# Combine rows behind every third gather instead of every second, with a small GpSimd write behind each gather

## What is computed

```python
x = x + 0.5 * ffn(layernorm(x))
x = x + attn(layernorm(x))          # einsum, softplus, exp, scan over time, einsum
x = x + 0.5 * ffn(layernorm(x))

def ffn(x):                          # 16 experts, 4 taken per token
    weights, indices = top_k(sigmoid(gate_w @ x) + gate_b, 4)
    weights = weights / weights.sum(-1)
    shared = silu(x @ w1s) * (x @ w3s) @ w2s
    for the four chosen experts e of a token:
        routed += weights[e] * (silu((x @ w1[e]) * (x @ w3[e])) @ w2[e])
    return shared + routed
```

## Time and profile before

| what | value |
|---|---|
| time, median of 3 runs | 590.1 us (585.19 to 593.1) |
| span of the profiled execution | 644.2 us |
| mean granted TensorE clock in it | 0.897 |
| busy: TensorE, VectorE, ScalarE, GpSimd | 517.4, 434.0, 376.0, 349.6 us |
| first and last x gather of loop 0 | 75.97 and 246.85 us |
| first and last x gather of loop 1 | 405.81 and 576.18 us |
| gathers issued by GpSimd | 158 of x, 64 early rows, 64 late rows |

### The profile page before, as it was taken

The page is one execution under the profiler, slowest core; times in us unless marked ns, Lnnn a source line. Parts: engine busy times, 40 slices in busy tenths (PEclk is TensorE's granted clock), DMA queues, the critical chain, the costliest instruction groups (busy, mean ns, idle before and its releaser), DMA issues.

```text
span 644.2 us, 13458 instructions
## 1 busy us (share of the span) xinstructions
PE 517.4 (80%) x3206; PEld 454.5 (71%) x3207; DVE 434.0 (67%) x1459; ACT 376.0 (58%) x1128; POOL 349.6 (54%) x364
## 2 busy tenths in 40 slices
PE   4976799999999999667586943799999899998460
PEld 3954589998888889455465931599988788887350
DVE  6798667767767677527686689467666667666434
ACT  2778466766657567555474664477766666665010
POOL 3899554456556565465311442544565556655764
PEclk9978589999999999697697975599999999999875
DMA  9971245565444445432100560254444454555644
GB/s 297 391 269 68 60 130 156 163 179 153 151 145 135 147 129 138 126 95 79 53 2 0 167 210 0 66 150 133 132 150 131 132 149 130 145 137 142 190 129 121
DMA packets 61149, 88.24 MB, mean 137 GB/s; under 512 B 9499, under 2 KB 46363, under 8 KB 61107
## 3 DMA queue, kind: packets, MB, share of 16 engines
q1 hardware_dynamic: 47379, 50.29, 22.7%
q0 software_dynamic: 13728, 37.50, 22.6%
HBM read 57.22 MB, written 30.54 MB: 136 GB/s over the span
## 4 chain that ended last, share of the span: by engine, by line
PE 56%; DVE 11%; issue 10%; ACT 9%; POOL 5%; another core or an unknown queue 4%; DMA 4%; SPq 1%; ACTq 0%; POOLq 0%; DVEq 0%
PE bank L1380 24%; PE bank L1431 10%; PE bank L1402 6%; POOL mamba_room L595 5%; PE bank L1442 4%; PE bank L1441 4%; PE bank L1599 2%; DMA ys_scratch<-ring_f 2%; PE bank L1488 2%; ACT ring_f L713 1%; ACT ring_r L664 1%; DVE xres L1159 1%; PE bank L1624 1%; PE bank L1453 1%
## 5 line engine op out<-in xcount | busy, mean ns | idle before, releaser
L560 POOL DMA_INDIRECT ring_f<-xn_scratch,tokidx x158 | 149.6, 947 | 153.0 <-PE bank L1402 100.6
L1380 PE MATMUL bank<-w_routed,ring_r 128*128 x948 | 195.5, 342 | 0.9 <-DVE ring_r L954 0.8
L1380 PEld LDWEIGHTS bank<-w_routed,ring_r 128*128 128x128 f32 x948 | 152.2, 192 | 6.6 <-issue 4.1
L1431 PE MATMUL bank<-w_routed,ring_r 128*128 x790 | 119.5, 281 | 3.0 <-ACT ring_f L692 2.1
L1431 PEld LDWEIGHTS bank<-w_routed,ring_r 128*128 128x128 f32 x790 | 110.0, 188 | 4.3 <-issue 4.3
L673 ACT ACTIVATE ring_r<-bank 128x256 fp32r<-128x256 f32 x158 | 60.7, 384 | 71.4 <-PE bank L1442 66.5
L962 DVE TENSOR_TENSOR ring_r<-bank,ring_r 128x128 fp32r<-128x128 f32 x158 | 45.6, 288 | 59.9 <-ACT ring_r L673 47.4
L595 POOL DMA_INDIRECT mamba_room<-ys_scratch,si x64 | 61.6, 962 | 29.1 <-issue 18.4
L954 DVE TENSOR_TENSOR ring_r<-bank,ring_r 128x256 fp32r<-128x256 f32 x158 | 67.1, 425 | 15.1 <-issue 5.4
L1402 PE MATMUL bank<-cst,ring_f 128*128 128x128 f32 x316 | 64.4, 286 | 10.0 <-DMA ring_f<-xn_scratch,tokidx 5.4
L682 ACT ACTIVATE stage<-bank 128x176 f32<-128x176 f32 x158 | 50.6, 320 | 35.7 <-remote 18.2
(11 more groups left out here) (172 smaller groups left out, 816.5 us busy)
## 6 DMA issues: line engine op xcount, KB each, us to landing
ys_scratch<-ring_f SPq DMA_DIRECT2D x158, 128.0 KB
raw_routed<-in_w13r SPq DMA_DIRECT2D x6, 704.0 KB, 12.5
xn_scratch<-w_routed SPq DMA_DIRECT2D x32, 128.0 KB, 4.9
raw_routed<-in_w2r SPq DMA_DIRECT2D x6, 512.0 KB, 12.8
raw_routed<-in_w13r SPq DMA_DIRECT2D x8, 352.0 KB, 6.4
ring_f<-xn_scratch,tokidx POOLq DMA_INDIRECT x158
xres<-in_x_in SPq DMA_DIRECT2D x4, 512.0 KB, 6.4
raw_routed<-in_w2r SPq DMA_DIRECT2D x8, 256.0 KB, 6.7
```

The lines of the kernel that those rows point to most:

```text
L560: pool.indirect_dma_start(xg[j % UN], None, xn_dram, bass.IndirectOffsetOnAxis(ap=tokidx[:, j:j + 1], axis=0)).then_inc(s_g[j % UN], 16)
L1380: last = pe.matmul(out, a, b, start=(q == 0), stop=(q == len(terms) - 1))
L1431: last = pe.matmul(p_y[b][:, 0:D], a, v, start=(q == 0), stop=(q == 4))
```

## The change

There are four parts.

1. `EARLY_TURN = 3`: early fetch n stands behind gather 29 + 3n instead of 29 + 2n.
2. `space`: from gather 25 on (`SPACED_FROM`), GpSimd writes 64 columns of zeros into `hid_room`, whose contents are no longer needed then, behind each x gather and behind each early fetch inside the loop. Each such write waits for the one before it, on a new semaphore that nothing else uses. Fetches behind the loop have none.
3. `MEASURED = 4`: one token tile fewer is measured inside the loop.
4. `measure_early` moves from the list's stage with lag 0 to that with lag 3, with the step number adjusted, so that it can still be reached in the steps after the last gather.

```diff
-EARLY_FIRST, EARLY_ADD = 29, 3
+EARLY_FIRST, EARLY_ADD, EARLY_TURN = 29, 3, 3
+SPACED_FROM, SPACE = EARLY_FIRST - 4, 64
-MEASURED = 5
+MEASURED = 4
...
-            return max(4 * (n // TOPK) + EARLY_FIRST, EARLY_FIRST + 2 * n)
+            return max(4 * (n // TOPK) + EARLY_FIRST, EARLY_FIRST + EARLY_TURN * n)
...
+            spaces = [0]
+
+            def space(j):
+
+                if j >= SPACED_FROM:
+                    if spaces[0]:
+                        pool.wait_ge(s_sp, spaces[0])
+                    spaces[0] += 1
+                    pool.memset(hid_room[:, 0:SPACE], 0.0).then_inc(s_sp, 1)
...
                 for j in range(NS):
                     gather(f, j)
+                    space(j)
                     for n in range(EARLY):
                         if early_after(n) == j:
                             fetch_early(f, n)
+                            space(j)
...
-                        if c == early_step(t * TOPK + TOPK - 1) + 1:
+                        if c + LAG_T + 1 == early_step(t * TOPK + TOPK - 1) + 1:
                             mark(measured(t))
-                    if f == 0 and c == early_step(SCALED[0][1] * TOPK - 1) + 3:
+                    if f == 0 and c + LAG_T + 1 == early_step(SCALED[0][1] * TOPK - 1) + 3:
...
-                                   (LAG_X, dve_x(base)), (LAG_X, shared_rows_first(f)), (LAG_X, measure_early(f))],
+                                   (LAG_X, dve_x(base)), (LAG_X, shared_rows_first(f)), (LAG_T + 1, measure_early(f))],
```

More of the change, by code:

```diff
@@ L296, in build @@
         s_ea = sem("early_added")
+        s_sp = sem("spaced")
         s_wo = sem("mamba_out_loaded")
```

## The result

| | median | lowest to highest | ratio to before (95% interval) |
|---|---|---|---|
| before | 590.88 us (4 runs) | 585.19 to 593.1 | |
| changed | 609.58 us (4 runs) | 607.54 to 611.89 | 1.0336 (1.0294 to 1.0377) |

The changed kernel is slower by 19 to 20 us. The forecast was 593 us, "that gain and loss nearly cancel", with 573 to 611 us as the range: the time lies inside the range, near its upper end, but outside the 582 to 602 us of the likeliest case. It lies 1.6 us from the 608 us of rival C.

The account below looks back on a forecast made before the run. Fetches in the loops were taken to make GpSimd's gathers delay TensorE's signals, 2.36 instead of 2.00 us per tile. Terms -19.7 + 20.0 + 2.0 + 0.4 = +2.7 on 590.1 gave 593 us, range 573 to 611 us.

Parts of the forecast that it names:

- likeliest case: Whole kernel: gain in the loops and loss behind them nearly cancel, 582 to 602 us; chance 0.38.
- rival C: Loops: late signals belong to the profiled execution, little to gain, eight more fetches behind each loop cost about +18, 608 us; chance 0.14.
- The pace of the loops, -19.7 us: Gathers 29 to 78, both loops: 2.16 instead of 2.36 us per tile, 9.5 and 10.2 us less.
- rival B: Loop rounds: zeros don't part the gathers, TensorE's signals stay held, the train of eight costs too; +20.5, 611 us; chance 0.16.
- GpSimd's 1.41 us per gather: GpSimd: a gather takes about 1.41 us though issued 1.25 us apart; three or more in succession delay TensorE's signals.
- the pace of 2.16 us per tile: Loops: GpSimd sets the pace, four gathers with zeros at 1.62 us each per three tiles.
- The zeros at 0.21 us: GpSimd in the loops: a write of 64 columns of zeros takes 0.21 us, between 0.10 and 0.54.
- The fetches behind the loops, +20.0 us: Behind each loop: eight more fetches in a row at 1.25 us, 10.0 us later each; not below 16.
- The train of eight at the loops' ends, +2.0 us: Each loop's end: gathers 77, 78 and fetches 16 to 21 hold TensorE's signals, up to 6 us, taken as 1 each.
- The one more statistic, +0.4 us: Behind loop 0: one more statistic is left to compute there, +0.4 us.
- A: Loops: spaced gathers keep signals prompt, zeros are short, 2.00 us per tile; -15.1, 575 us; chance 0.29.
- D: Loops: zeros take 0.54 us or more, GpSimd holds 2.60 us per tile; +24 + 20, 634 us; chance 0.03.

Follow-up runs that it names:

- before_again: The kernel before, unchanged, profiled a second time: 590.86 us, ratio 1.0035.
- before_third: The kernel before, unchanged, profiled a third time: 592.11 us (1 run).
- open_all: The kernel before with fetch n behind gather 29 + 5n/3 and, in layer 1, no fetch waits for TensorE's tiles or shared sums: 578.76 us, ratio 0.9782.

## Why the prediction went as it did

**The pace of the loops, -19.7 us: wrong, it was nothing.** The rows were read rightly: in that execution TensorE's signals were late. The step that failed is the last one of the sum, "Carried over as it is, the forecast is 590.1 + 2.7". The span was 54 us above the median, the late signals in the loops were 35.5 us, and this was weighed as rival C with 0.14. It should have been the likeliest: a loss of 54 us in one execution has to sit somewhere, and the prediction had found one that filled most of it and whose cause, signals that come late, no instruction of the program asks for. before_again and before_third show the loops of the same kernel at 98.3 to 98.4 us, 2.01 us per tile, and in the changed kernel the sign that was named for this term, 100 to 110 us, didn't come (98.5 and 98.2 us). So nothing was there to gain. That 609.58 us lies inside the range of 573 to 611 us is luck: its upper end stood there for rival B, which didn't come, and the forecast itself, that gain and loss nearly cancel, failed by this term.

**GpSimd's 1.41 us per gather: wrong as a rule of the kernel.** It described that execution, and not all of it: three at 1.41 us are 4.2 us, and the loop took 4.7 us for two tiles. In the others three gathers in a row, and 32 in a row at the end of the kernel, go out at 1.25 us and TensorE's signals come as they do without gathers (0.31 us from transpose to copy). With it falls the pace of 2.16 us per tile: gather and zeros take 1.28 us, not 1.62.

**The zeros at 0.21 us: near (0.17 us).** They cost nothing, since they stand in the 0.30 us between two issues. In the Trainium skill ("GPSIMD Engine Reference", "2.1 Instruction dispatch") consecutive Pool instructions are no barrier between the engine's cores. Whether the zeros would have parted the gathers all the same no run here shows: without late signals there was nothing for them to part. Rival B's 611 us came near the time for the wrong reason.

**The fetches behind the loops, +20.0 us: right.** Measured are 19 to 20 us for 16 fetches, about 10 us at each end, by the steps given: rooms that come free only behind the loop, nine in a row instead of one, then VectorE, ScalarE and TensorE behind loop 0, and the late fetches behind loop 1. The first late fetch comes 27.8 us behind the last x gather of loop 0 where it came 19.0 us behind it in before_again, and 26.8 us where it came 17.2 us in loop 1: 8.7 and 9.5 us, for the 10 us forecast. The lower bound of 16 us, by GpSimd's idle time, wasn't needed.

**The train of eight at the loops' ends, +2.0 us: nothing,** since no signal is held. The one more statistic, +0.4 us, is below what the runs tell apart.

**The rivals.** C came, at 608 us for 609.58: its loops were at TensorE's pace already, and the fetches stood behind them unhidden. A was right on the changed kernel's loops, 2.00 us per tile, but before had them as well. D's 2.60 us per tile is out (and by its own terms its 24 us are 23.4).

## What to carry to other kernels

Hold the span of the profiled execution against the timed runs before any row of it is priced: where it is 9% longer, the excess has a place, and a change that removes what stands at that place may remove nothing from the timed runs. A second profile of the same kernel settles it. And a gather moved from a loop in which its engine has room to a place behind it cost its full issue time there (1.2 to 1.3 us each, with 8 and 16 more), where its buffer came free only behind the loop. Fewer than 7 behind the loop gained nothing until the waits that ended next were gone too: rooms alone 1.000, tiles and sums alone 1.001, rooms and tiles 0.995, all three 0.978.

## What was not expected

Two executions of the same program on the chip differ by 55 us, and in the longer one TensorE's signals came late behind the third gather of a round (1.08 us where it is 0.31 us otherwise). What sets off that execution is open: it wasn't seen again in the profiles of the eleven other kinds of run, with rounds of three and more gathers in a row, with and without zeros, nor in two more profiles of the same kernel. Whether the zeros or the turn of 3 would guard against it was therefore not tried.

In the other profiles trains of gathers held no such signals. open_all issues 32 late fetches at 1.25 us, beginning beside the loop's last tiles, and its x gathers 29 to 78 stay at 98.9 to 99.0 us. From gather 29 to the last matmuls with w2 its loop 1 takes 115.4 us, where the two ordinary profiles of before have 113.9 and 113.2; no run tells whether the train costs these 2 us.
